# Node degrees of a graph layer as rows out of wide matmuls, in place of columns that are turned and copied

## The chip, the cores and the metric

The kernel runs on one core of a Trainium2 chip. The metric is device time in microseconds (us) of one execution. A change of 0.3% (2.3 us) either way is about what can be told from none.

## What is computed

3125 nodes with 256 features, 50,000 edges sorted by destination, and a layer norm with relu ahead of four SAGE layers:

```python
def _sage_conv(x, src, dst, Wl, Wr, b):
    n = x.shape[0]
    agg = jax.ops.segment_sum(x[src], dst, num_segments=n)
    deg = jax.ops.segment_sum(jnp.ones_like(dst, dtype=x.dtype), dst, num_segments=n)
    mean = agg / jnp.maximum(deg, 1.0)[:, None]
    return mean @ Wl + x @ Wr + b
...
h = jnp.maximum(_layernorm(x, axis=-1), 0.0)
x = x + gnn(h)      # relu after layers 1, 2 and 3
```

The change concerns `1 / maximum(deg, 1)`, which each layer multiplies into the summed neighbours.

## The kernel before

The edges are turned into a dense matrix `counts` (source by destination), kept in SBUF as 25 source tiles of 128 partitions with one column for each destination node. The sum over neighbours is then a matmul: `H` (two fp16 parts of the features) is the stationary operand, 512 columns of `counts` the moving one (`add_sources`, L1617).

Destinations are worked on in seven chunks, here called places q = 0 to 6. The order is written out by hand (`ORDER` = 5, 6, 4, 3, 2, 1, 0): place 0 is a chunk of 512 nodes, place 1 the last 53 nodes, places 2 to 6 have 512 nodes each. In layer 1 the matrix is built while it is used: in places 0 and 2 to 5, `script(q)` mixes two kinds of work over source tiles k = 0 to 24. One is the neighbour sum of this place (four 512-column matmuls for each k). The other is the building of `counts` for later places: VectorE (DVE) makes one-hot tables in pairs of instructions (`step`, L1061), TensorE (PE) multiplies them into `window_ps` (L1517), ScalarE (ACT) copies the result into `counts` (L1288). There are two buffers of tables (`GROUPS = 2`), so DVE can be at most two groups ahead of PE. Every engine works through its own list in the order in which it is written, and the engines meet at semaphores. Place 6 builds nothing.

The degrees of a place are made in four steps, before the sums of that place are scaled:

- `add_degrees` (PE, L1637): for each 128 nodes of the place, 25 matmuls with 128 columns of `counts` as the stationary operand and two columns of ones as the moving one. The result is a column in `lin_ps`. It is 100 matmuls for a place of 512 nodes and stands ahead of everything else in the place.
- `degrees` (DVE, L1143 and L1145): maximum with 1 and reciprocal on 128 partitions by 4, into `rdeg_columns`. PE waits for it at k = 1 (`degree_inverted`).
- `turn_degrees` (PE, L1649): four fp32 matmuls (two passes each, eight records) against an identity spread the columns over all partitions as rows in `degree_ps`, at k = 12 (k = 20 in place 0).
- `copy_degrees` (ACT, L1312): `degree_ps` to `rdeg`, 128 by 512.

In place 0, `degrees(0)` stands on DVE behind `choose_rest` (L907, tables of chosen steps) and far ahead of the steps. Near the end of layer 1 the DMA queue of SP stores the seven column tiles to `rdeg_d` in DRAM (`store_rdeg`, L609), and layers 2 to 4 load them from there as rows, spread over the partitions. `scale_agg` (L1117) multiplies by `rdeg`. In `script` terms, `lin` of the place before stands at k = 2, `narrow` at 10, `turn` at 18.

Of the kernel before, what the change touches and what calls it, by code (L numbers as in the profile page):

```python
# [26 lines left out]
def sage_stack_kernel(nc, x, src, dst, Wl1, Wr1, b1, Wl2, Wr2, b2, Wl3, Wr3, b3, Wl4, Wr4, b4, out):  # L27
# [13 lines left out]
    P = 128  # L41
# [3 lines left out]
    NT = -(-N // P)  # L45
    TAIL = N - (NT - 1) * P
    TPC = 4
# [153 lines left out]
    with ctx:  # L201
# [54 lines left out]
        norm_parts = uppers[:, 0:2 * NCH * TPC].rearrange("p (a c t) -> p a c t", a=2, c=NCH)  # L256
        rdeg_columns = uppers[:, 2 * NCH * TPC:3 * NCH * TPC].rearrange("p (q t) -> p q t", t=TPC)
        ident32 = uppers[:, 3 * NCH * TPC:3 * NCH * TPC + P]
# [160 lines left out]
        degree_inverted = sem("degree_inverted")  # L419
        degree_turned = sem("degree_turned")  # L420
        late_loaded = sem("late_loaded")
        rdeg_made = sem("rdeg_made")
        rdeg_stored = sem("rdeg_stored")
# [73 lines left out]
        REST_AT = {1: (0, 4, 9), 2: (0, 8), 3: (0, 7, 11)}  # L497
        DEGREE_TURN_K, DEGREE_COPY_K = 12, 13
        LIN_K, NARROW_K, TURN_K = 2, 10, 18
# [40 lines left out]
        def _(sp):  # L540
# [46 lines left out]
            for l in (1, 2, 3, 4):  # L587
# [17 lines left out]
                def store_rdeg(q):  # L605
                    c = ORDER[q]
                    n, t = size_of(c)
                    rows_ = P if n == CH else n
                    sp.dma_start(rdeg_d[0, c * CH:c * CH + n].rearrange("(t p) -> p t", p=rows_),  # L609
                                 rdeg_columns[0:rows_, q, 0:t], allow_slow_non_contiguous=True  # L610
                                 ).then_inc(rdeg_stored, 16)

# [69 lines left out]
                with sp.Fori(2, NCH - 2) as q:  # L682
                    after(q)
                if l == 1:
                    sp.wait_ge(degree_inverted, NCH)
                    for q in range(NCH):
                        store_rdeg(q)
                after(NCH - 2)
# [144 lines left out]
        def _(dve):  # L833
# [270 lines left out]
            def scale_agg(l, q, bank):  # L1104

                n, t = size_of(chunk_at(q))
                if l > 1:
                    dve.wait_ge(rdeg_loaded[l], 16 * (q + 1))
                else:
                    dve.wait_ge(rdeg_made, q + 1)  # L1110
                    if q == 0:
                        wait_h0T(dve)
# [26 lines left out]
            def degrees(q):  # L1139
                n, t = size_of(chunk_at(q))  # L1140
                rows_ = P if n == CH else n
# [90 lines left out]
        def _(act):  # L1232
# [159 lines left out]
            for q in range(NCH):  # L1392
# [3 lines left out]
                for kind, k in script(q):  # L1396
# [21 lines left out]
                    if q == 0 and k == 22:  # L1418
                        root_row(1)
                    if k == (DEGREE_COPY_K if q else FIRST_TURN_K + 1):  # L1420
                        copy_degrees(q)
                    if q >= 1 and k == RELU_K:
# [20 lines left out]
        def _(pe):  # L1443
# [179 lines left out]
            def add_degrees(q):  # L1623

                c = chunk_at(q)
                n, t = size_of(c)
                rows_ = P if n == CH else n
                if q == 0:
                    pe.wait_ge(h0T_copied, 8)
                elif q == 1:  # L1630
                    pe.wait_ge(h0T_copied, 2 * NCH)
                    pe.wait_ge(norms_made, 3)
                else:
                    pe.wait_ge(low_done[1], q - 1)
# [6 lines left out]
            def turn_degrees(q):  # L1641

                n, t = size_of(chunk_at(q))
                rows_ = P if n == CH else n
                pe.wait_ge(degree_inverted, q + 1)
                if q >= 1:
                    pe.wait_ge(rdeg_made, q)
                for i in range(t):
                    last = m(degree_ps[:, i * P:i * P + rows_], rdeg_columns[0:rows_, q, i:i + 1].broadcast_to([rows_, P]),  # L1649
                             ident32[0:rows_, 0:rows_], start=True, stop=True)  # L1650
                last.then_inc(degree_turned, 1)

# [22 lines left out]
            for q in range(NCH):  # L1675

                pe.wait_ge(window_stored, filled_after(q - 1))
                add_degrees(q)
                if q >= 1:
                    pe.wait_ge(agg_scaled[1], 2 * q)  # L1680
                for kind, k in script(q):
# [4 lines left out]
                    if kind != "sum":  # L1686
                        continue
                    if k == 1:
                        pe.wait_ge(degree_inverted, q + 1)
                    if q == 0 and k % TPC == 0:  # L1690
# [78 lines left out]
```

## Time and profile before

| | us |
|---|---|
| runs shown: median of 3 (lowest, highest) | 767.74 (765.6, 768.23) |
| profiled execution, its own time | 772.98 |
| its span, first to last instruction | 771.2 |
| mean granted TensorE clock | 0.944 |
| PE busy | 684.8 |
| DVE busy | 273.1 |
| ACT busy | 173.3 |
| POOL busy | 49.1 |

Busy time says how much an engine did, not what limited the kernel: the chain of waits (which work released which) and the stretches with their granted clock tell that. A granted clock of 1.00 is TensorE at 2.4 GHz, one of 0.50 is 1.2 GHz. Layer 1 lasts from about 66 to 399 us, layers 2 to 4 the rest.

### The profile page before, as it was taken

Reading aid. Unit: us, or ns where it says so; the run is one execution under the profiler, and the core shown is the slowest. Engines: PE = TensorE matmul, PEld = TensorE weight load, DVE = VectorE, ACT = ScalarE, POOL = GpSimd, SP = SyncE. Lnnn points to the kernel's source line nnn. Section 1 sums busy time; section 2 is a strip of 40 time slices with the busy share of each in tenths; the row PEclk is TensorE's granted clock in tenths of the full one; section 3 lists DMA queues with packets and bytes.
Section 4 is the critical chain, followed back from the end, with each engine's and each line's share of the span. In section 5 each row is a group of like instructions: output and inputs, shape, how many; then the busy total and the mean of one; then the engine's idle time right before and its main releaser. Section 6 shows DMA issues by size and latency. Waiting matters only on the chain.

```text
span 771.2 us, 11223 instructions
## 1 busy us (share of the span) xinstructions
PE 684.8 (89%) x4513; PEld 369.2 (48%) x4514; DVE 273.1 (35%) x627; ACT 173.3 (22%) x339; POOL 49.1 (6%) x91
## 2 busy tenths in 40 slices
PE   2637967899999999999996999989998999999997
PEld 1314544465555455455443444344443556466464
DVE  6696168168366475570101122122122101101001
ACT  4455166235163261130011001111211000000000
POOL 6213110000000000000000000000000101100100
PEclk9965989799899899999996999999999999999999
DMA  8011000010010100105342323422245330330230
GB/s 253 10 55 56 28 31 28 32 45 4 2 55 15 53 4 15 55 15 11 91 148 74 108 74 126 150 88 90 82 136 198 123 106 1 95 96 0 95 95 28
DMA packets 39422, 53.48 MB, mean 69 GB/s; under 512 B 8557, under 2 KB 21518, under 8 KB 39376
## 3 DMA queue, kind: packets, MB, share of 16 engines
q1 hardware_dynamic: 39260, 52.59, 22.4%
q8 instruction: 33, 0.54, 0.3%
q10 hardware_dynamic: 116, 0.24, 0.1%
q14 instruction: 13, 0.11, 0.0%
HBM read 31.86 MB, written 20.97 MB: 68 GB/s over the span
## 4 chain that ended last, share of the span: by engine, by line
PE 76%; DVE 13%; DMA 4%; ACT 3%; issue 2%; SPq 1%; DVEq 0%; POOL 0%; ACTq 0%; POOLq 0%
PE agg_ps L1617 35%; PE window_ps L1617 12%; PE lin_ps L1587 10%; PE window_ps L1517 6%; DVE early L1061 6%; PE lin_ps L1571 6%; PE lin_ps L1637 2%; PE turn_ps L1606 2%; PE lin_ps L1595 1%; DMA H_d<-newH 1%; DMA H<-H_d 1%; PE agg_ps L1663 1%; DVE counts L883 1%; ACT counts L1288 1%; PE window_ps L1454 1%
## 5 line engine op out<-in xcount | busy, mean ns | idle before, releaser
L1617 PE MATMUL agg_ps<-counts,H 128*128 128x512 f16 (+2 forms) x1500 | 361.6, 377 | 5.0 <-DMA H<-H_d 2.2
L1617 PEld LDWEIGHTS agg_ps<-counts,H 128*128 128x128 f16 x1500 | 130.3, 100 | 126.9 <-issue 13.9
L1061 DVE TENSOR_TENSOR early<-early 128x768 f16<-128x768 bf16 (+5 forms) x318 | 141.8, 500 | 69.7 <-PE window_ps L1517 68.5
L1517 PE MATMUL window_ps<-early 128*128 128x100 f16 (+1 forms) x892 | 101.8, 225 | 49.3 <-DVE early L1061 37.5
L1288 ACT ACTIVATE counts<-window_ps 128x400 f16<-128x400 f32 x196 | 97.1, 506 | 138.6 <-PE window_ps L1517 134.8
L1517 PEld LDWEIGHTS window_ps<-early 128*128 128x128 f16 x892 | 67.7, 102 | 125.8 <-issue 41.2
L1617 PE MATMUL window_ps<-counts,H 128*128 (+1 forms) x600 | 96.7, 317 | 0.0
L1617 PEld LDWEIGHTS window_ps<-counts,H 128*128 128x128 f16 x600 | 46.1, 99 | 49.5 <-issue 4.1
L800 POOL TENSOR_TENSOR newH<-newH,early 128x256 f32<-128x256 f32 (+1 forms) x25 | 17.4, 727 | 631.7 <-DMA newH<-in_x_dram 631.7
L1117 DVE SCALAR_TENSOR_TENSOR aggT<-agg_ps,columns,rdeg 128x512 f32<-128x512 f32 (+1 forms) x30 | 20.6, 716 | 97.2 <-PE agg_ps L1617 81.8
L1327 ACT ACTIVATE newT<-lin_ps,columns 128x512 f32<-128x512 f32 (+1 forms) x28 | 17.4, 633 | 120.8 <-PE lin_ps L1587 120.8
L1136 DVE COPY newH<-turn_ps 128x1024 f16<-128x1024 f16 (+1 forms) x28 | 17.7, 632 | 58.8 <-PE turn_ps L1606 58.8
L1124 DVE SCALAR_TENSOR_TENSOR partsT<-newT,columns,partsT 128x512 f16<-128x512 f32 (+1 forms) x21 | 14.3, 683 | 53.8 <-ACT partsT L1338 53.3
L1587 PE MATMUL lin_ps<-selfT,early 128*128 128x512 f32 (+1 forms) x56 | 26.8, 583 | 5.9 <-DMA W<-in_L_gnn_Wr_dram 4.9
L1207 DVE TENSOR_TENSOR newT<-lin_ps,newH 128x512 f32<-128x512 f32 (+1 forms) x13 | 8.7, 670 | 55.4 <-PE lin_ps L1571 55.4
L1571 PE MATMUL lin_ps<-W,aggT 128*128 128x256 f32 (+1 forms) x100 | 25.9, 382 | 1.7 <-DVE aggT L1117 1.7
L1587 PE MATMUL lin_ps<-aggT,W 128*128 128x512 f32 (+1 forms) x56 | 26.1, 590 | 1.2 <-DVE aggT L1117 1.2
L1571 PE MATMUL lin_ps<-W,selfT 128*128 128x256 f32 (+1 forms) x100 | 25.7, 379 | 0.0
L1587 PE MATMUL lin_ps<-selfT,W 128*128 128x512 f32 (+1 forms) x56 | 23.8, 547 | 0.0
L1327 ACT ACTIVATE newT<-newT,columns 128x512 f32<-128x512 f32 (+1 forms) x7 | 4.7, 667 | 84.0 <-DVE newT L1219 84.0
L1606 PE MATMUL turn_ps<-ident,partsT 128*128 128x128 f16 (+1 forms) x200 | 16.7, 227 | 5.4 <-DVE partsT L1124 5.4
L1571 PEld LDWEIGHTS lin_ps<-W,aggT 128*128 128x128 f32 (+1 forms) x100 | 18.5, 187 | 5.7 <-DVE aggT L1117 2.3
(138 smaller groups left out, 377.6 us busy)
## 6 DMA issues: line engine op xcount, KB each, us to landing
selfT<-hT_d SPq DMA_DIRECT2D x18, 512.0 KB, 4.3
hT_d<-newT SPq DMA_DIRECT2D x14, 512.0 KB, 4.1
rdeg<-rdeg_d SPq DMA_DIRECT2D x18, 256.0 KB, 4.2
counts<-in_x_dram SPq DMA_DIRECT2D x6, 512.0 KB, 6.9
H_d<-newH SPq DMA_DIRECT2D x12, 256.0 KB, 2.0
H<-H_d SPq DMA_DIRECT2D x12, 256.0 KB, 4.0
H_d<-newH SPq DMA_DIRECT2D x6, 512.0 KB, 2.6
H<-H_d SPq DMA_DIRECT2D x6, 512.0 KB, 5.2
```

What stands on the lines that cost most here:

```text
L800: nc.gpsimd.tensor_tensor(x4[0:q, i, :], x4[0:q, i, :], b4rows[0:q, :], ALU.add).then_inc(x4_biased, 1)
L1061: last = v.tensor_tensor(hot[:, group % GROUPS, 0:n * size].rearrange("p (r n d) -> p r n d", r=n, d=2), numbers_to[:, 0:size].rearrange(" ...
L1117: v.scalar_tensor_tensor(out=aggT[:, h, 0:n], in0=(agg_ps, window_ps)[bank][:, h, 0:n], scalar=unscale[:, l - 1:l], in1=rdeg[:, 0:n], op0= ...
L1136: v.tensor_copy(to, turn_ps[0:rows_, 0:2 * t, :].rearrange("p (t a) f -> p t a f", a=2)).then_inc(turn_copied[l], 1)
L1288: a.activation(counts[:, :, 2 * w * WIN:2 * (w + 1) * WIN].rearrange("p t (a w) -> p a t w", a=2), window_ps[:, FILL_AT[w] % 2, 0:2 * KEYS ...
L1327: a.activation(newT[:, h, 0:n], source, ACT.Relu, bias=bT[:, bias + h:bias + h + 1]).then_inc(relu_done[l], 1)
L1517: m(window_ps[:, at % 2, key0:key0 + keys], hot_src[:, group % GROUPS, r * P:(r + 1) * P], hot_key[:, group % GROUPS, r * keys:(r + 1) * k ...
L1571: last = m(lin_ps[0:rows_, g, i * D:(i + 1) * D], h, w, start=(j == 0), stop=(j == len(ops) - 1))
L1587: last = m(lin_ps[:, h, 0:n], w, r, start=(i == 0), stop=(i == len(ops) - 1))
L1606: last = nc.tensor.transpose(turn_ps[0:rows_, 2 * i + part, :], partsT[:, part, i * P:i * P + rows_], ident16[:, :])
L1617: last = m((agg_ps, window_ps)[bank][:, h, 0:n], H_of[:, k, part, h * P:(h + 1) * P], counts[:, k, chunk_cols(c, n)], start=first and part ...
L1637: last = m(lin_ps[0:rows_, 0, 2 * i:2 * i + 2], counts[:, k, bass.ds((c * TPC + i) * P, rows_)], ones16[:, 0:2], start=(k == 0), stop=(k = ...
```

## The change

`add_degrees` now has a 128 by 128 block of ones as the stationary operand and 512 columns of `counts` (53 in place 1) as the moving one. So every partition of `degree_ps` gets the whole row of degrees, with 25 matmuls for a place. `turn_degrees` and `copy_degrees` are gone, and so are PE's waits for `degree_inverted` at k = 1. `degrees` on DVE reads 128 by 512 from `degree_ps` and writes 128 by 512 into `rdeg`, the maximum and the reciprocal both on that shape. Since there is one `rdeg`, it first waits for the store of the row before it. In place 0 both the matmuls and the two DVE instructions stand at k = 20. The stores to `rdeg_d` are one row each and are issued place by place.

```diff
             def degrees(q):
                 n, t = size_of(chunk_at(q))
-                rows_ = P if n == CH else n
                 dve.wait_ge(degree_done, q + 1)
-                order.after(v.tensor_scalar(rdeg_columns[0:rows_, q, 0:t], lin_ps[0:rows_, 0, 0:2 * t].rearrange(
-                    "p (t a) -> p t a", a=2)[:, :, 0], 1.0, None, ALU.max))
-                v.reciprocal(rdeg_columns[0:rows_, q, 0:t], rdeg_columns[0:rows_, q, 0:t]).then_inc(degree_inverted, 1)
+                if q > 0:
+                    dve.wait_ge(rdeg_stored, 16 * q)
+                    dve.wait_ge(agg_scaled[1], 2 * q)
+                order.after(v.tensor_scalar(rdeg[:, 0:n], degree_ps[:, 0:n], 1.0, None, ALU.max))
+                v.reciprocal(rdeg[:, 0:n], rdeg[:, 0:n]).then_inc(degree_inverted, 1)
...
                     choose_rest()
-                    degrees(0)
                     h0_shift(5)
...
-                    if q >= 1 and k == DEGREE_K:
+                    if k == (DEGREE_K if q else FIRST_TURN_K):
                         degrees(q)
...
-            def copy_degrees(q):
-                n, t = size_of(chunk_at(q))
-                act.wait_ge(degree_turned, q + 1)
-                if q > 0:
-                    act.wait_ge(agg_scaled[1], 2 * q)
-                a.activation(rdeg[:, 0:n], degree_ps[:, 0:n], ACT.Copy).then_inc(rdeg_made, 1)
...
-                for i in range(t):
-                    for k in range(NT):
-                        last = m(lin_ps[0:rows_, 0, 2 * i:2 * i + 2], counts[:, k, bass.ds((c * TPC + i) * P, rows_)],
-                                 ones16[:, 0:2], start=(k == 0), stop=(k == NT - 1))
+                for k in range(NT):
+                    last = m(degree_ps[:, 0:n], ones16[:, 0:P], counts[:, k, chunk_cols(c, n)], start=(k == 0),
+                             stop=(k == NT - 1))
                 last.then_inc(degree_done, 1)
...
-                    if k == 1:
-                        pe.wait_ge(degree_inverted, q + 1)
...
-                    if k == (DEGREE_TURN_K if q else FIRST_TURN_K):
-                        turn_degrees(q)
+                    if q == 0 and k == FIRST_TURN_K:
+                        add_degrees(q)
...
                 def after(q, last=False):
 
+                    if l == 1:
+                        store_rdeg(q)
                     sp.wait_ge(lin_done[l], both(q + 1, LIN[l], 1 if l == 4 else LIN[l]))
```

On PE, at the start of place 0, the block of 100 matmuls stands ahead of the first sums. Before:

```order
L1552 ISA
L1637 MATMUL lin_ps<-newH,counts 128x2 x100
L1617 MATMUL agg_ps<-counts,H 128x512 x32
L1481 MATMUL lin_ps<-newH,counts 128x128 x8
L1617 MATMUL agg_ps<-counts,H 128x512 x4
```

Now:

```order
L1535 ISA
L1600 MATMUL agg_ps<-counts,H 128x512 x32
L1464 MATMUL lin_ps<-newH,counts 128x128 x8
L1600 MATMUL agg_ps<-counts,H 128x512 x4
```

The sums come first (L1617 of before is L1600 now), and the degree block has moved to k = 20, below.

On DVE, in the last third of place 0, six rows of one-hot tables (each pair is one group) and then `bound_h2` (`counts<-counts`). Before:

```order
L1061 TENSOR_TENSOR early<-early 128x768
L1061 TENSOR_TENSOR early<-early 128x600
L1061 TENSOR_TENSOR early<-early 128x768
L1061 TENSOR_TENSOR early<-early 128x600
L1061 TENSOR_TENSOR early<-early 128x768
L1061 TENSOR_TENSOR early<-early 128x600
L1016 TENSOR_SCALAR counts<-counts 128x128
```

Now:

```order
L1053 TENSOR_TENSOR early<-early 128x768
L1053 TENSOR_TENSOR early<-early 128x600
L1137 TENSOR_SCALAR rdeg<-degree_ps 128x512
L1138 RECIPROCAL rdeg<-rdeg 128x512
L1053 TENSOR_TENSOR early<-early 128x768
L1053 TENSOR_TENSOR early<-early 128x600
L1053 TENSOR_TENSOR early<-early 128x768
L1053 TENSOR_TENSOR early<-early 128x600
L1008 TENSOR_SCALAR counts<-counts 128x128
```

The two degree instructions now stand ahead of the last two groups and of everything behind them. PE's block of 25 stands at the same point, behind the first half of k = 20.

On PE, at the turn from place 1 to place 2 (as at the starts of places 3 to 5). Before:

```order
L1606 MATMUL turn_ps<-ident,partsT 128x128 x8
L1617 MATMUL agg_ps<-counts,H 128x53 x26
L1637 MATMUL lin_ps<-newH,counts 128x2 x100
L1617 MATMUL agg_ps<-counts,H 128x512 x2
L1517 MATMUL window_ps<-early 128x100 x4
```

Now:

```order
L1589 MATMUL turn_ps<-ident,partsT 128x128 x8
L1600 MATMUL agg_ps<-counts,H 128x53 x26
L1616 MATMUL degree_ps<-counts,newH 128x512 x25
L1600 MATMUL agg_ps<-counts,H 128x512 x2
L1500 MATMUL window_ps<-early 128x100 x4
```

The block keeps its place and changes its kind. Behind it PE has two matmuls of its own, and then needs a table from DVE, whose list has the two degree instructions first.

## Rows read from the trace of the kernel before

**Rows 1.** The page, busy us and share of the span, by engine.

```profile
PE 684.8 (89%) x4513; PEld 369.2 (48%) x4514; DVE 273.1 (35%) x627; ACT 173.3 (22%) x339; POOL 49.1 (6%) x91
```

**Rows 2.** Chain of waits, start of layer 1: start us, us, what.

```profile
66.38 5.49 DVE counts L907 x16
...
72.21 8.44 PE agg_ps L1617 x28
```

**Rows 3.** Timeline of PE there: start us, us, what, idle before and releaser.

```profile
66.54 2.80 PE L1637 MATMUL lin_ps<-newH,counts 128*128 128x2 f16 x100 [0.83 <-ACT newT L1267]
```

**Rows 4.** Windows: stretch, its us, busy by engine, then granted clock, DMA, GB/s.

```profile
76.00:78.00 2.00, 2.00 (x9) 0.89 (x8) 0.00 (x0) 0.00 (x0) 2.00 (x4) 0.81 0.00 0
```

**Rows 5.** Chain of waits, from place 1 into place 2.

```profile
156.09 2.49 PE lin_ps L1637 x100
...
158.98 0.84 DVE early L1061 x2
...
159.95 0.49 PE window_ps L1517 x4
```

**Rows 6.** Chain of waits, place 6.

```profile
369.81 0.89 PE degree_ps L1649 x8
370.70 5.18 PE agg_ps L1617 x24
```

**Rows 7.** Groups of DVE by shape: count, busy us, mean ns, idle before.

```profile
L1001 DVE TENSOR_TENSOR counts<-counts 128x256 f32<-128x256 f32 x2 | 0.8, 424 | 0.1
...
L1001 DVE TENSOR_TENSOR counts<-counts 128x128 f32<-128x128 f32 x1 | 0.3, 291 | 0.0
...
L1145 DVE RECIPROCAL newH<-newH 128x4 f32<-128x4 f32 x6 | 1.1, 178 | 0.2
...
L874 DVE RECIPROCAL newH<-newH 128x1 f32<-128x1 f32 x1 | 0.2, 165 | 2.4 <-ACT newH L1246 2.4
...
L1145 DVE RECIPROCAL newH<-newH 53x1 f32<-53x1 f32 x1 | 0.2, 155 | 0.0
```

**Rows 8.** One line's instructions: count, min, median, max ns, first and last start.

```profile
L874 DVE RECIPROCAL newH<-newH x7: 157/177/179, 13.3 to 100.8; 128x4 f32<-128x4 f32 x6, 128x1 f32<-128x1 f32 x1
```

**Rows 9.** Windows behind the degree blocks of places 2 to 5.

```profile
157.50:163.50 6.00, 5.29 (x71) 3.20 (x67) 3.89 (x10) 1.84 (x4) 0.00 (x0) 0.72 0.05 16
199.80:206.80 7.00, 6.42 (x37) 3.28 (x35) 3.89 (x10) 2.02 (x4) 0.00 (x0) 0.52 0.01 2
250.50:258.00 7.50, 6.70 (x37) 3.36 (x34) 3.89 (x10) 1.01 (x2) 0.00 (x0) 0.54 0.00 1
298.00:304.50 6.50, 5.50 (x114) 3.92 (x112) 3.94 (x10) 0.00 (x0) 0.00 (x0) 0.81 0.01 3
```

**Rows 10.** Timeline, last third of place 0, DVE.

```profile
121.56 1.92 DVE L1061 TENSOR_TENSOR early<-early 128x768 f16<-128x768 bf16 x4 [0.96 <-PE window_ps L1517]
123.39 0.28 DVE L1016 TENSOR_SCALAR counts<-counts 128x128 f32<-128x128 f32 x1
```

**Rows 11.** Timeline, last third of place 0, PE.

```profile
122.77 1.05 PE L1649 MATMUL degree_ps<-newH 128*128 128x128 f32 x8
```

**Rows 12.** Timeline of PE, an idle stretch ahead of place 0's steps.

```profile
103.62 0.82 PE L1517 MATMUL window_ps<-early 128*128 128x200 f16 x4 [4.61 <-DVE early L1061]
```

**Rows 13.** Windows, that stretch: the slices in which the clock changed.

```profile
100.00:101.00 1.00, 0.00 (x0) 0.00 (x0) 0.21 (x2) 0.63 (x2) 0.48 (x1) 0.82 0.00 0
107.00:108.00 1.00, 1.00 (x8) 0.88 (x7) 0.00 (x0) 0.51 (x2) 0.00 (x0) 0.77 0.00 0
```

**Rows 14.** Chain of waits, place 1.

```profile
139.57 1.31 PE lin_ps L1637 x25
...
141.38 0.45 PE agg_ps L1617 x6
```

**Rows 15.** Timeline of DVE, end of place 5, and of SP's queue behind it.

```profile
341.68 0.68 DVE L1136 COPY newH<-turn_ps 128x1024 f16<-128x1024 f16 x1
...
350.92 3.70 SPq L609 DMA_DIRECT2D rdeg_d<-newH  x7
```

More of the change, by code:

```diff
@@ L256, in sage_stack_kernel @@
         norm_parts = uppers[:, 0:2 * NCH * TPC].rearrange("p (a c t) -> p a c t", a=2, c=NCH)
-        rdeg_columns = uppers[:, 2 * NCH * TPC:3 * NCH * TPC].rearrange("p (q t) -> p q t", t=TPC)
         ident32 = uppers[:, 3 * NCH * TPC:3 * NCH * TPC + P]
@@ L419, in sage_stack_kernel @@
         degree_inverted = sem("degree_inverted")
-        degree_turned = sem("degree_turned")
         late_loaded = sem("late_loaded")
-        rdeg_made = sem("rdeg_made")
         rdeg_stored = sem("rdeg_stored")
@@ L497, in sage_stack_kernel @@
         REST_AT = {1: (0, 4, 9), 2: (0, 8), 3: (0, 7, 11)}
-        DEGREE_TURN_K, DEGREE_COPY_K = 12, 13
         LIN_K, NARROW_K, TURN_K = 2, 10, 18
@@ L605, in store_rdeg @@
                 def store_rdeg(q):
-                    c = ORDER[q]
+                    c = chunk_at(q)
                     n, t = size_of(c)
-                    rows_ = P if n == CH else n
-                    sp.dma_start(rdeg_d[0, c * CH:c * CH + n].rearrange("(t p) -> p t", p=rows_),
-                                 rdeg_columns[0:rows_, q, 0:t], allow_slow_non_contiguous=True
-                                 ).then_inc(rdeg_stored, 16)
+                    sp.wait_ge(degree_inverted, q + 1)
+                    sp.dma_start(rdeg_d[0:1, chunk_cols(c, n)], rdeg[0:1, 0:n]).then_inc(rdeg_stored, 16)
                 def store_new(q):
@@ L683, in _ @@
                     after(q)
[L684 to L687, printed above, removed]
                 after(NCH - 2)
@@ L1109, in scale_agg @@
                 else:
-                    dve.wait_ge(rdeg_made, q + 1)
+                    dve.wait_ge(degree_inverted, q + 1)
                     if q == 0:
@@ L1140, in degrees @@
                 n, t = size_of(chunk_at(q))
-                rows_ = P if n == CH else n
                 dve.wait_ge(degree_done, q + 1)
-                order.after(v.tensor_scalar(rdeg_columns[0:rows_, q, 0:t], lin_ps[0:rows_, 0, 0:2 * t].rearrange(
-                    "p (t a) -> p t a", a=2)[:, :, 0], 1.0, None, ALU.max))
-                v.reciprocal(rdeg_columns[0:rows_, q, 0:t], rdeg_columns[0:rows_, q, 0:t]).then_inc(degree_inverted, 1)
+                if q > 0:
[3 more added lines that the diff above has]
+                v.reciprocal(rdeg[:, 0:n], rdeg[:, 0:n]).then_inc(degree_inverted, 1)
             for i, w in enumerate(FILLS[-1]):
@@ L1419, in _ @@
                         root_row(1)
-                    if k == (DEGREE_COPY_K if q else FIRST_TURN_K + 1):
-                        copy_degrees(q)
                     if q >= 1 and k == RELU_K:
@@ L1626, in add_degrees @@
                 n, t = size_of(c)
[L1627 to L1630, printed above, removed]
+                if q > 0:
+                    pe.wait_ge(degree_inverted, q)
+                if q == 1:
                     pe.wait_ge(h0T_copied, 2 * NCH)
                     pe.wait_ge(norms_made, 3)
-                else:
-                    pe.wait_ge(low_done[1], q - 1)
-                for i in range(t):
-                    for k in range(NT):
-                        last = m(lin_ps[0:rows_, 0, 2 * i:2 * i + 2], counts[:, k, bass.ds((c * TPC + i) * P, rows_)],
-                                 ones16[:, 0:2], start=(k == 0), stop=(k == NT - 1))
-                last.then_inc(degree_done, 1)
-            def turn_degrees(q):
-                n, t = size_of(chunk_at(q))
-                rows_ = P if n == CH else n
-                pe.wait_ge(degree_inverted, q + 1)
[L1646 to L1651, printed above, removed]
+                for k in range(NT):
+                    last = m(degree_ps[:, 0:n], ones16[:, 0:P], counts[:, k, chunk_cols(c, n)], start=(k == 0),
+                             stop=(k == NT - 1))
+                last.then_inc(degree_done, 1)
             for i, w in enumerate(FILLS[-1]):
@@ L1677, in _ @@
                 pe.wait_ge(window_stored, filled_after(q - 1))
-                add_degrees(q)
+                if q == 0:
+                    pe.wait_ge(h0T_copied, 8)
                 if q >= 1:
+                    add_degrees(q)
                     pe.wait_ge(agg_scaled[1], 2 * q)
@@ L1687, in _ @@
                         continue
-                    if k == 1:
-                        pe.wait_ge(degree_inverted, q + 1)
                     if q == 0 and k % TPC == 0:
@@ L1705, in _ @@
                     add_sources(1, q, 0, k, k == 0, k == NT - 1, halves=(0,))
-                    if k == (DEGREE_TURN_K if q else FIRST_TURN_K):
-                        turn_degrees(q)
+                    if q == 0 and k == FIRST_TURN_K:
+                        add_degrees(q)
                     if q >= 1 and k == LIN_K:
```

## The prediction, made before the changed kernel ran

> **What bounds the kernel now.** I read the page first. PE is busy for 684.8 of 771.2 us and DVE for 273.1 [rows 1], but that is a mean over stages. The changed code lives in layer 1 alone, so I then followed the chain of waits from 60 to 400 us, and the timeline and the windows with their granted clock wherever the chain met a degree instruction. Five spots matter.
>
> *Start of place 0.* PE does the 100 small matmuls from 66.54 [rows 3], the four sums of k = 0, and then stands until DVE has done `choose_rest` (5.49 us from 66.38) and, behind it, `degrees(0)`. Only at 72.21 does PE go on with 28 sums, which take 8.44 us to 80.65 [rows 2]. The clock is at 1.2 GHz at first. In the window from 76 to 78 its mean is 0.81 [rows 4], so it rose at about 76.76 (0.5 for 0.76 us, 1.0 for 1.24).
>
> *Last third of place 0.* DVE sets the pace. It starts the groups that stand where the change inserts at 121.56 and the bounds behind them at 123.39, with no wait between [rows 10]. PE reaches k = 20 and turns the degrees at 122.77 [rows 11].
>
> *Starts of places 2 to 5.* Here both engines follow one another on the chain: degree block 2.49 us from 156.09 (to 158.58), DVE's two small instructions, a group of tables from 158.98, and PE's first step at 159.95 [rows 5]. The other three places read alike. Later in such a place PE is the fuller engine.
>
> *Place 6.* It builds nothing and PE is its bound: block, sums, and 0.89 us of turning, all on the chain [rows 6].
>
> *The clock.* Behind the degree blocks of places 2 to 5 it falls to 1.2 GHz. From the mean clocks 0.72, 0.52, 0.54 and 0.81 over 6.0, 7.0, 7.5 and 6.5 us [rows 9] the time at half speed is twice the missing share: 3.4, 6.7, 6.9 and 2.5 us, 19.5 in all. What PE did before each fall: 2.5 us of two-column matmuls and then some 0.6 to 1 us of waiting.
>
> **The change, part by part.**
>
> *The block of matmuls.* 24 sums of 512 columns take 5.18 us at full clock [rows 6], 0.216 each. The new block has 25 of that shape: 5.40 us against 2.49, so +2.91 in each place with 512 nodes. In place 1 (53 columns) I take old and new as equal.
>
> *The turning* goes: 8 records, −0.89 us on PE [rows 6], in the middle of a place where PE is the bound, so I credit it in full. ACT's copy goes as well. ACT waits for PE most of the time, so 0.
>
> *The maximum on 128 by 512.* An fp32 instruction of DVE goes from 291 ns at 128 columns to 424 at 256 [rows 7]: 1.04 ns a column over a base of 0.16 us, so 0.69 us for 512.
>
> *The reciprocal on 128 by 512* is the disputed price. No row shows it wide. Lower bound: a column costs it what it costs the instruction above, 0.69 us. Upper bound: L1145 goes from 155 ns at one column to 178 at four [rows 7], 7.7 ns a column, so 0.155 + 511 × 0.0077 = 4.1 us. L874 goes from 165 ns at one column [rows 7] to a median of 177 [rows 8], 4.0 ns a column and 2.2 us. These are differences of 12 and 23 ns, so weak, but both are well above 1.04. I take the mean slope, 5.85: 3.15 us.
>
> *Places 2 to 5.* What stands behind DVE's reciprocal is the first group of tables, and PE waits for that with only two sums of its own in hand. Block end to group start was 158.98 − 158.58 = 0.40 us [rows 5]. Now it is 0.69 + 3.15 + 0.07 for three hand-overs = 3.91, so +3.51. With +2.91 and −0.89 a place grows by 5.53; four: +22.1.
>
> *The last third of place 0.* PE reaches k = 20 at 122.77 and its block ends at 128.17. DVE's degree instructions then end at 132.06 or so. The groups that began at 121.56 [rows 10] begin 10.5 us later. DVE has no slack behind them, so +10.5. If the reciprocal is cheap (0.69), it is 8.0.
>
> *The start of place 0.* PE no longer does the block there and waits for nothing of DVE before k = 9, which needs `choose_rest` (71.87 at the latest, as now). So 32 sums start at 66.54. The clock rose 4.55 us after PE began to work without a pause (72.21 to 76.76). The same from 66.54 gives 71.09: 10.65 sums at 0.427 us, 21.35 at 0.216, end at 75.70 against 80.65: −4.95. Bounds: the rise stays at 76.76 (−2.1), or full clock from the first (−7.2). All that follows to 103 us hangs on PE's chain, so the gain is kept.
>
> *Place 1.* PE's wait at k = 1 goes: block end 140.88 to 141.38 [rows 14], −0.5.
>
> *Place 6.* +2.91 − 0.89 = +2.0. The reciprocal is hidden here: DVE is needed next only at k = 14. Were that cover gone, it would cost its 3.9 us.
>
> *The clock.* PE now has 4.5 us of waiting behind each block. There is one such row: PE stood for 4.61 us until 103.62 [rows 12], the clock fell at 100.64 and rose at 107.46 (from 0.82 and 0.77 in their slices [rows 13]), so 3.84 us at half speed after work began again, a loss of 1.9. Today's loss in places 2 to 5 is about (19.5 minus some 3 of waiting) / 2 / 4 = 2.1 each. So no change there, and +0.9 for place 0, which gets such a stretch for the first time, half of it under DVE.
>
> *The stores.* DVE now waits, before it overwrites `rdeg`, for the store of the row before it. SP issues that behind the store that follows `copy_turned`, at 341.68 in place 5, 8.8 us before `degrees(6)` [rows 15]; place 1 is tighter, but the block is now 5.4 us and covers it. 0. A store that landed later than that would hold DVE, and then PE, by the difference. The seven scattered stores (3.70 us of SP's queue, [rows 15]) had nothing behind them on SP but a wait for `lin` of place 5, which PE does only after that. 0.
>
> Sum: −4.95 + 10.5 + 0.9 − 0.5 + 22.1 + 2.0 = +30.05 us. The profiled execution would go from 773.0 to 803. It lies 0.7% above the median of the runs shown, 767.7, and on the median the sum gives 797.8.
>
> **The rivals.**
>
> *The reciprocal is as cheap as a copy.* Then DVE's part is 2.46 shorter in five places, and PE waits only 2 us behind each block, which is now full-width work, so that the clock may stay up: −4.95 + 8.0 − 0.5 + 4 × 3.07 + 2.0 = +16.8, and −8.3 for the clock (4 × 2.1): +8.5, 776; 784 if the clock falls all the same. For it: a pipeline that overlaps its passes. Against: both slopes of rows 7 and 8.
>
> *The reciprocal costs 4.1 to 4.4 and the clock stays down longer.* +1.0 to +1.25 in five places, and +1 in each for the clock: 808. For it: the slope of L1145. Against: that of L874.
>
> *The change is faster.* Mechanism: the clock. The wide block keeps it up behind all four blocks (−8.3) and through place 1, which starts at 1.2 GHz today (−2.3). It decides only if DVE's two instructions also lie fully under PE's work, so that just PE's terms are left: five places × 2.02 and 4.5 in place 0 = 14.6. With −4.95 and −0.5: −1.5, 766. Against it: in places 2 to 5 PE has 0.43 us of work of its own behind the block, and DVE's cheapest case is 1.45.
>
> *No net change*: the same without place 1, 768.
>
> **How the numbers follow.** Chances: forecast (797.8) 0.70, own range 789 to 804; longer reciprocal 0.12; cheap reciprocal 0.13 and the same without the clock's help 0.02; faster 0.02; no change 0.01. The range 776 to 806 leaves out most of the longer case and the last two. A change under 0.3%, 2.3 us, can't be told from none. Faster 0.02, same 0.01, slower 0.97.
>
> **What the new profile would show.** Right: RECIPROCAL 128 by 512 near 3.1 us; the block 25 times 0.216; PE idle for about 4.5 us behind it in places 2 to 5, released by the tables; the sums at the start of place 0 without a pause and the matmuls of the first select (L1454 of before) 5 us earlier; the bounds in the last third of place 0 about 5.5 us later than now (10.5 less the lead). Wrong: a reciprocal of 0.7 us, or a clock at 1.00 behind the blocks, or DVE waiting for a DMA ahead of its maximum.

## The result, and the profile after

The changed kernel takes 800.5 us (median of 4, 799.7 to 803.1) against 766.7: ratio 1.044, 95% interval 1.041 to 1.047, so +33.8 us. The forecast was 797.8 and +30. The profiled execution took 799.72 us with a span of 797.9.

The page of the changed kernel, part 1 (busy time by engine):

```profile
PE 693.8 (87%) x4013; PEld 362.2 (45%) x4014; DVE 294.5 (37%) x627; ACT 170.4 (21%) x332; POOL 49.1 (6%) x91
```

Against [rows 1], PE has 9.0 us more and DVE 21.4 more. Neither sum tells what the 33.8 us are. The groups of DVE by shape do half of it (count, busy us, mean ns, idle before):

```profile
L1138 DVE RECIPROCAL rdeg<-rdeg 128x512 f32<-128x512 f32 x6 | 20.1, 3353 | 0.2
L1137 DVE TENSOR_SCALAR rdeg<-degree_ps 128x512 f32<-128x512 f32 x6 | 4.2, 692 | 30.2 <-PE degree_ps L1616 30.2
L1138 DVE RECIPROCAL rdeg<-rdeg 128x53 f32<-128x53 f32 x1 | 0.5, 490 | 0.0
```

The reciprocal takes 3.353 us where I had 3.15. From 53 to 512 columns it is (3353 − 490) / 459 = 6.24 ns a column, six times the 1.04 ns of [rows 7]. The maximum takes 0.692, the forecast to the digit. DVE stood 30.2 us ahead of the maxima, waiting for PE's blocks.

The chain of waits from place 1 into place 2 answers to [rows 5]:

```profile
160.03 5.41 PE degree_ps L1616 x25
165.46 0.70 DVE rdeg L1137
166.19 3.35 DVE rdeg L1138
169.54 0.80 DVE early L1053 x2
170.47 0.49 PE window_ps L1500 x4
```

All three new terms are on it, one behind the other: block 5.41, maximum 0.70, reciprocal 3.35, and only then the first group of tables that PE waits for. PE's timeline at the same spot shows the wait:

```profile
170.47 0.49 PE L1500 MATMUL window_ps<-early 128*128 128x100 f16 x4 [4.62 <-DVE early L1053]
```

The last third of place 0, timeline of DVE, against [rows 10]:

```profile
123.12 0.69 DVE L1137 TENSOR_SCALAR rdeg<-degree_ps 128x512 f32<-128x512 f32 x1 [7.76 <-PE degree_ps L1616]
123.85 3.35 DVE L1138 RECIPROCAL rdeg<-rdeg 128x512 f32<-128x512 f32 x1
127.12 1.72 DVE L1053 TENSOR_TENSOR early<-early 128x768 f16<-128x768 bf16 x4
128.76 0.28 DVE L1008 TENSOR_SCALAR counts<-counts 128x128 f32<-128x128 f32 x1
```

DVE stands 7.76 us and then works 4.04 on degrees. And the start of place 0, timeline of PE, against [rows 2, 3]:

```profile
64.67 9.53 PE L1600 MATMUL agg_ps<-counts,H 128*128 128x512 f16 x32 [0.88 <-ACT newT L1259]
74.04 1.04 PE L1464 MATMUL lin_ps<-newH,counts 128*128 128x128 f32 x8
```

The 32 sums run in one go. The windows behind the blocks of places 2 to 5 (stretch, busy by engine, then granted clock, DMA share, GB/s) answer to [rows 9]:

```profile
168.00:176.50 8.50, 6.03 (x35) 4.04 (x36) 5.05 (x9) 2.01 (x4) 0.00 (x0) 0.60 0.00 0
219.50:224.00 4.50, 4.50 (x24) 2.50 (x22) 2.31 (x6) 2.01 (x4) 0.00 (x0) 0.62 0.01 4
274.00:278.50 4.50, 3.50 (x23) 2.10 (x24) 3.24 (x9) 0.50 (x1) 0.00 (x0) 0.62 0.00 0
328.50:333.50 5.00, 4.44 (x26) 2.60 (x27) 3.14 (x8) 0.00 (x0) 0.00 (x0) 0.66 0.00 0
```

By twice the missing share they hold 6.8, 3.4, 3.4 and 3.4 us at 1.2 GHz, 17.0 in all. For the kernel before, the prediction read 19.5 from [rows 9]. The last of those windows ends too early: in place 5 the clock is still down behind it (0.69 from 304.5 to 306), so it was 3.4 us there, not 2.5, and some 20.5 in all.

Measured from block to block (and in place 6 to the start of the last `lin`), the places took, before and after: place 0 73.0 and 79.55, place 1 16.5 and 15.8, place 2 41.4 and 48.7, place 3 50.7 and 55.8, place 4 49.65 and 54.1, place 5 50.1 and 55.7, place 6 35.2 and 37.2. Together that is 316.6 and 346.9 us, +30.3 in layer 1.

### The profile page after: what moved, and what is told of

It is laid out like the page before. It is cut to its first block, busy times and chain, and to the rows that moved or that the text cites. A ratio compares the mean times of both kernels' runs of the same rounds, so it can differ in the third digit from the quotient of the medians.

```text
span 797.9 us, 10217 instructions
## 1 busy us (share of the span) xinstructions
PE 693.8 (87%) x4013; PEld 362.2 (45%) x4014; DVE 294.5 (37%) x627; ACT 170.4 (21%) x332; POOL 49.1 (6%) x91
## 4 chain that ended last, share of the span: by engine, by line
PE 76%; DVE 14%; ACT 3%; DMA 2%; issue 2%; POOL 1%; SPq 1%; ACTq 0%; DVEq 0%; POOLq 0%
PE agg_ps L1600 34%; PE window_ps L1600 11%; PE lin_ps L1570 9%; DVE early L1053 6%; PE lin_ps L1554 5%; PE window_ps L1500 5%; PE degree_ps L1616 4%; DVE rdeg L1138 2%; PE turn_ps L1589 2%; PE lin_ps L1578 1%; POOL counts L709 1%; DMA H_d<-newH 1%; ACT counts L1280 1%; PE lin_ps L1464 1%; DVE counts L875 1%
## 5 line engine op out<-in xcount | busy, mean ns | idle before, releaser
L1600 PE MATMUL agg_ps<-counts,H 128*128 128x512 f16 (+2 forms) x1500 | 360.0, 376 | 4.1 <-DMA H<-H_d 1.8
L1600 PEld LDWEIGHTS agg_ps<-counts,H 128*128 128x128 f16 x1500 | 131.0, 100 | 126.0 <-issue 15.0
L1600 PE MATMUL window_ps<-counts,H 128*128 (+1 forms) x600 | 96.2, 316 | 0.0
L1600 PEld LDWEIGHTS window_ps<-counts,H 128*128 128x128 f16 x600 | 45.6, 98 | 49.6 <-issue 4.1
L1109 DVE SCALAR_TENSOR_TENSOR aggT<-agg_ps,columns,rdeg 128x512 f32<-128x512 f32 (+1 forms) x30 | 20.5, 715 | 96.8 <-PE agg_ps L1600 81.6
L1128 DVE COPY newH<-turn_ps 128x1024 f16<-128x1024 f16 (+1 forms) x28 | 17.7, 632 | 56.6 <-PE turn_ps L1589 56.6
L1616 PE MATMUL degree_ps<-counts,newH 128*128 128x512 f16 (+1 forms) x175 | 34.6, 357 | 1.6 <-issue 1.6
L1116 DVE SCALAR_TENSOR_TENSOR partsT<-newT,columns,partsT 128x512 f16<-128x512 f32 (+1 forms) x21 | 14.3, 683 | 54.1 <-ACT partsT L1323 53.6
L1554 PE MATMUL lin_ps<-W,selfT 128*128 128x256 f32 (+1 forms) x100 | 25.7, 379 | 0.0
L1616 PEld LDWEIGHTS degree_ps<-counts,newH 128*128 128x128 f16 x175 | 15.8, 101 | 19.5 <-issue 2.0
```

The source lines that it names most:

```text
L1109: v.scalar_tensor_tensor(out=aggT[:, h, 0:n], in0=(agg_ps, window_ps)[bank][:, h, 0:n], scalar=unscale[:, l - 1:l], in1=rdeg[:, 0:n], op0= ...
L1128: v.tensor_copy(to, turn_ps[0:rows_, 0:2 * t, :].rearrange("p (t a) f -> p t a f", a=2)).then_inc(turn_copied[l], 1)
L1554: last = m(lin_ps[0:rows_, g, i * D:(i + 1) * D], h, w, start=(j == 0), stop=(j == len(ops) - 1))
L1600: last = m((agg_ps, window_ps)[bank][:, h, 0:n], H_of[:, k, part, h * P:(h + 1) * P], counts[:, k, chunk_cols(c, n)], start=first and part ...
L1616: last = m(degree_ps[:, 0:n], ones16[:, 0:P], counts[:, k, chunk_cols(c, n)], start=(k == 0), stop=(k == NT - 1))
```

## The experiments

**1. The kernel before once more.** The profiled execution of before lay 6 us above the median of its runs, so 3.5 us of the measured 33.8 had no place in the comparison above.

> The kernel before once more, unchanged, with a profile of its own. Its profiled execution (772.98 us) lay 6 us above the median of its runs (766.7), while that of the changed kernel lay at its median. Theory: the extra 4 to 6 us is spread between executions (head of the program, clock), so a new profile near 767 should show layer 1 from PE's first sum to the last agg scaled within 2 us of the 317 us of the first profile, and the rest elsewhere. Rival: the first profile had an extra stall inside layer 1, and then the new one shows layer 1 shorter by 3 to 6 us, so that the change costs more there than the 30.2 us that the two profiles show. Time against before: same, 766 to 768.

Measured: 766.9 us, ratio 1.000 (0.997 to 1.003). Its profile has a span of 766.4, and layer 1 takes 313.4 us, not 316.6. The rival holds: the first profile had 3.2 us more inside layer 1. Windows of this profile, behind the blocks of places 2 to 5:

```profile
155.00:162.00 7.00, 6.35 (x132) 4.39 (x128) 4.04 (x12) 1.32 (x3) 0.00 (x0) 0.76 0.12 40
196.00:205.00 9.00, 8.00 (x135) 5.22 (x133) 5.21 (x12) 2.01 (x4) 0.00 (x0) 1.00 0.02 5
247.00:255.00 8.00, 7.00 (x55) 3.83 (x52) 3.89 (x10) 1.01 (x2) 0.00 (x0) 0.79 0.01 3
295.00:303.00 8.00, 7.00 (x83) 4.29 (x81) 3.89 (x10) 0.00 (x0) 0.00 (x0) 0.79 0.00 0
```

In place 3 the clock did not fall at all, and in place 4 for 3.4 us in place of 6.9: 10.1 us at half speed against some 20.5 in the first profile, with the same program. Places 2 to 5 took 41.4, 48.4, 48.7 and 50.0 us here (41.4, 50.7, 49.65 and 50.1 in the first profile). Against this profile the change costs 33.5 us in layer 1, close to the 33.8 of the medians.

**2. Without the reciprocal.** The values are then not means.

```diff
-                v.reciprocal(rdeg[:, 0:n], rdeg[:, 0:n]).then_inc(degree_inverted, 1)
+                v.tensor_scalar(rdeg[:, 0:n], rdeg[:, 0:n], 0.001, None, ALU.min).then_inc(degree_inverted, 1)
```

> The changed kernel with the wide reciprocal (3.353 us) replaced by a wide minimum with 0.001 on the same tile, so the scaled values are not the means; everything else is as it was. Theory (the reciprocal is on the path in places 0 and 2 to 5): the wide minimum takes about 0.43 us, so 2.9 less in five places, -14.6: 786 us. If PE's shorter wait (about 2 us in place of 5) also keeps its clock at 2.4 GHz behind the blocks, about 7 us more are gained: 779. Rival (the wait behind the block is not the reciprocal's but the tables', or the time comes back as a wait elsewhere): 797 to 801.

Measured: 779.1 us, 21.4 less than the changed kernel (ratio to before 1.016, 1.010 to 1.022). The wide minimum takes 0.426 us, so 2.93 less in each of five places, 14.6. Most of the other 6.8 goes with the clock: in the profiles, places 2 to 5 are 17.7 us shorter together, 11.7 of which is the reciprocal, and the remaining 5.9 come where 17.0 us at 1.2 GHz are gone. Windows of this run behind the same four blocks:

```profile
163.00:169.50 6.50, 4.75 (x42) 3.17 (x40) 4.61 (x10) 2.01 (x4) 0.00 (x0) 1.00 0.00 0
206.50:213.50 7.00, 5.19 (x33) 2.60 (x32) 4.61 (x10) 2.01 (x4) 0.00 (x0) 1.00 0.01 2
258.00:265.00 7.00, 5.19 (x32) 2.61 (x31) 4.61 (x10) 1.01 (x2) 0.00 (x0) 1.00 0.01 4
308.00:315.00 7.00, 4.93 (x32) 2.46 (x31) 4.61 (x10) 0.00 (x0) 0.00 (x0) 1.00 0.00 0
```

The clock is at 1.00 throughout. So this run is close to the case that the prediction called the cheap reciprocal (776): its second instruction is cheaper still, 0.43 and not 0.69, and it comes out 3 us above that.

**3. A block of 12 source tiles.** The degrees are then too small.

```diff
-                for k in range(NT):
+                for k in range(12):
...
-                             stop=(k == NT - 1))
+                             stop=(k == 11))
```

> The changed kernel with the degree block cut to 12 of its 25 source tiles, so the degrees are too small; the DVE instructions are the same. 12 matmuls of 512 columns take 2.6 us, as long as the old block. Theory (PE's block is on the path in all six places of 512 nodes): -2.8 in each, -16.8 in all: 784 us. Rival (in places 0 and 2 to 5 the block is covered, because DVE has table groups left to build): -2.8 in place 6 alone: 797.

Measured: 784.5 us, 16.0 less than the changed kernel (ratio to before 1.023, 1.017 to 1.029). 13 matmuls of 0.216 us in six places are 16.8. In the profiles the six places are shorter by 2.7, 3.1, 3.0, 1.8, 2.8 and 2.8 us, so the block is on the path everywhere, not in place 6 alone. (In the one with 1.8, place 4, this run has 6.8 us at 1.2 GHz and the changed kernel 3.4.)

**4. Place 0's inverse at the end of the place.**

```diff
                     if kind == "summed":
+                        if q == 0:
+                            degrees(0)
                         scale_agg(1, q, 0)
...
-                    if k == (DEGREE_K if q else FIRST_TURN_K):
+                    if q >= 1 and k == DEGREE_K:
```

> The changed kernel with the two DVE degree instructions of place 0 moved from k = 20 to the end of place 0, just ahead of the scaling of its sums; PE's block stays at k = 20. Theory (at k = 20 DVE stands 7.8 us for PE's block and then works 4.1 us at the degrees, while PE has nothing to do, and this costs 10.6 us): now DVE goes on while the block runs, is late by the block alone (4.5 us net of the turning that went), and the 4.1 us come back at the end of the place, partly under PE's block of place 1: 8 us in place of 10.6, so -2 to -4: 797 to 798.5. Rival (DVE sets the pace in all of the last third of place 0, so where the work stands makes no difference): within 1 us of 800.5.

Measured: 794.5 us, 6.0 less than the changed kernel, more than I expected. Place 0 takes 73.3 us, what it took before the change. The timeline of DVE in this run shows why:

```profile
117.04 1.91 DVE L1053 TENSOR_TENSOR early<-early 128x768 f16<-128x768 bf16 x4 [0.96 <-PE window_ps L1502]
118.87 0.28 DVE L1008 TENSOR_SCALAR counts<-counts 128x128 f32<-128x128 f32 x1
...
124.54 1.80 DVE L1053 TENSOR_TENSOR early<-early 128x768 f16<-128x768 bf16 x4 [3.06 <-PE window_ps L1502]
```

DVE has built its two groups at about 118.9, just as PE begins its block (118.24 to 123.8), goes through the bounds beneath the block, and so stands for 3.06 us, not 7.76. I had counted the block as a full delay of DVE and forgotten the 2.6 us of bounds that fit beneath it. Of the reciprocal, 2.82 us come back as PE's wait ahead of the block of place 1.

**5. The start lead alone, on the kernel before.** The gain at the start of place 0 does not need wide rows.

```diff
-                add_degrees(q)
                 if q >= 1:
+                    add_degrees(q)
                     pe.wait_ge(agg_scaled[1], 2 * q)
...
-                    if k == 1:
+                    if k == 1 and q > 0:
                         pe.wait_ge(degree_inverted, q + 1)
+                    if q == 0 and k == 14:
+                        pe.wait_ge(degree_inverted, 1)
...
                     if q == 0 and k == FIRST_STEPS_K:
+                        add_degrees(0)
                         pe.wait_ge(step_tables, 4)
...
                     choose_rest()
-                    degrees(0)
...
                     more_tables(2)
+                    degrees(0)
```

> The kernel before with one edit: the 100 small matmuls of place 0 and the wait for them leave the start of place 0 and stand at k = 13, where PE waits 4.6 us for DVE's first tables; DVE's two small degree instructions stand behind the last step tables. Theory (the start lead of the changed kernel, 4.6 us, comes only from PE's missing block and wait, and does not need wide rows): 766.5 - 4.6 = 762 us, with PE's first sums running without a pause. Rival (the lead is lost again, because the clock falls on the small matmuls or DVE is held up ahead of the first tables): 765 to 767.

Measured: 763.2 us against 767.1 (ratio 0.994, 0.992 to 0.997), faster than both kernels: 3.9 of the expected 4.6 us. PE's timeline in this run:

```profile
65.48 8.55 PE L1617 MATMUL agg_ps<-counts,H 128*128 128x512 f16 x32
...
90.26 2.64 PE L1637 MATMUL lin_ps<-newH,counts 128*128 128x2 f16 x100
97.00 0.83 PE L1517 MATMUL window_ps<-early 128*128 128x200 f16 x4 [3.65 <-DVE early L1061]
```

The block lies where PE waits for DVE anyway, and PE still waits 3.65 us behind it, so it costs nothing there. This edit is in runs 6, 9 and 10 as well.

**6. The small block spread over the place.** Run 5, and the 100 small matmuls of places 1 to 6 in ten parts:

```diff
-        LOW_K, DEGREE_K, COPY_K = 14, 0, 20
+        LOW_K, DEGREE_K, COPY_K = 14, 11, 20
...
                 if q >= 1:
-                    add_degrees(q)
                     pe.wait_ge(agg_scaled[1], 2 * q)
...
-                    if k == 1 and q > 0:
-                        pe.wait_ge(degree_inverted, q + 1)
...
+                    if q >= 1 and k < SPREAD:
+                        some_degrees(q, k)
```

> As e5_block0_in_gap, and in places 1 to 6 the block of small matmuls no longer stands ahead of the place but is spread in ten parts over k = 0 to 9, into the free bank degree_ps; DVE's two small instructions stand at k = 11 and nothing waits at k = 1. Theory (at the start of a place the small block costs more than its 2.5 us of PE: DVE stands through it, PE then waits for tables, and the clock falls to 1.2 GHz for 3.4 to 6.8 us in most places): about 1 us less of waiting and 1 to 1.5 us less for the clock in each of places 2 to 5, -8 to -10 against e5_block0_in_gap: 753 us. Rival (the small matmuls cost more between large ones, or DVE waits at k = 11 instead): 760 to 763.

Measured: 766.8 us (ratio 0.999, 0.997 to 1.001), 14 more than the theory said. The small matmuls are hardly dearer (ten take 0.25 us from the first to the next large one, as in the block; only the first ten of places 2 to 5 take 0.42), and the clock stays at 1.00 in places 2 to 5. Two other things ate the gain. First, timeline of PE at the start of place 6 (it is the same at the starts of places 3, 4 and 5, and 0.69 us in place 2):

```profile
337.06 0.59 PE L1619 MATMUL agg_ps<-counts,H 128*128 128x512 f16 x2 [1.26 <-DVE aggT L1118]
```

PE now waits for the scaling of the place before, which the block had covered: 5.7 us in the five places. From scaling to scaling, places 2 to 5 are 4.7 us shorter than in run 5, where 8 to 10 were expected, and place 6 is 1.5 longer. Second, the end of place 6 (timeline, SP's queue and PE):

```profile
355.37 3.43 SPq L610 DMA_DIRECT2D rdeg_d<-newH  x7
...
358.84 0.58 SPq L597 DMA_DIRECT2D selfT<-hT_d  x1
...
377.61 2.90 PE L1589 MATMUL lin_ps<-aggT,W 128*128 128x512 f32 x3 [6.29 <-DMA selfT<-hT_d]
```

The seven scattered stores now stand directly ahead of the load of `selfT`, since `degree_inverted` comes later in place 6, and that load took 18.6 us to land. PE stood 6.3 us for it.

**7. The wide reciprocal in pieces.** The changed kernel, maximum at k = 3 and eight pieces at k = 4 to 18 in places 2 to 6:

```diff
+            def invert(q, i):
+                cols = slice(i * CH // 8, (i + 1) * CH // 8)
+                last = v.reciprocal(rdeg[:, cols], rdeg[:, cols])
...
+                    if q >= 2 and k % 2 == 0 and 4 <= k <= 18:
+                        invert(q, k // 2 - 2)
```

> The changed kernel, but in places 2 to 6 the maximum stands at k = 3 and the reciprocal is cut into eight pieces of 64 columns at k = 4, 6, ... 18, between the groups of tables. A piece should take 0.16 + 64 x 0.00624 = 0.56 us, 4.5 us in all. Theory (DVE is idle for some 17 us of such a place, so pieces that are shorter than the two groups it may be ahead are covered): 4 us less in four places, and PE waits only for the first tables, so the clock stays up, about 7 us more: 777 us. Rival (DVE's lead is too short, PE waits for each piece): 795 to 802.

Measured: 778.6 us, 21.9 less than the changed kernel. The forty pieces take 0.538 us each, 21.0 us in all, more than the 16.8 of the five whole reciprocals that they replace, and are covered. DVE's busy time is 292.7 us, almost that of the changed kernel, so it was never the amount of work that cost, but its place. The maximum moved along with the reciprocal, and the clock stays at 1.00 in places 2 to 5, so the 21.9 are worth all three together.

**8. The wide reciprocal under the next block.** The changed kernel, reciprocal at the end of places 0 and 2 to 5, and a semaphore of its own for PE once the maximum is through:

```diff
                     if kind == "summed":
+                        if q not in (1, NCH - 1):
+                            invert(q)
                         scale_agg(1, q, 0)
...
-                    if k == (DEGREE_K if q else FIRST_TURN_K):
+                    if k == {0: 22, 1: 0}.get(q, 3):
...
-                    pe.wait_ge(degree_inverted, q)
+                    pe.wait_ge(degree_read, q)
```

> The changed kernel, but in places 0 and 2 to 5 the reciprocal stands at the end of the place, just ahead of the scaling, and the maximum at k = 3 (k = 22 in place 0); PE's next block waits only until the maximum has read degree_ps. Theory (3.35 us of reciprocal and 1.4 us of scaling fit under the next block of 5.4 us, which stood idle for DVE before): 4 us less in four places and 7 us less for the clock, and 6 to 8 us less in place 0, as in e4_place0_inverse_last and with no wait of place 1's block: 770 to 772 us. Rival (the time comes back at the end of the place, because the scaling and lin behind it are now late): 785 to 795.

Measured: 768.3 us (ratio to before 1.001, 0.999 to 1.003), 32 less than the changed kernel, and no different from the kernel before. The three parts of the edit (reciprocal, maximum, semaphore) were not run one by one. Timeline at the start of place 3:

```profile
191.64 3.34 DVE L1145 RECIPROCAL rdeg<-rdeg 128x512 f32<-128x512 f32 x1
...
194.44 5.56 PE L1625 MATMUL degree_ps<-counts,newH 128*128 128x512 f16 x25
195.02 1.41 DVE L1110 SCALAR_TENSOR_TENSOR aggT<-agg_ps,columns,rdeg 128x512 f32<-128x512 f32 x2
...
196.35 1.78 DVE L1054 TENSOR_TENSOR early<-early 128x768 f16<-128x768 bf16 x4
199.84 0.59 PE L1609 MATMUL agg_ps<-counts,H 128*128 128x512 f16 x2
```

The scaling and the first two groups of tables lie under the block and are done by 198.13, and PE goes from its block to the next sum at 199.84 without a wait. The reciprocal lies mostly ahead of the block: 2.8 of its 3.34 us pass while PE still does the last sums of place 2 (191.64 to 194.44), and 2.0 to 2.8 us at the ends of places 3 to 5. So the theory had the cover in part wrong: the last sums of a place cover the reciprocal, which the early semaphore allows, and the block covers what follows it.

**9. Run 6 with the stores place by place.**

```diff
+                    if l == 1:
+                        sp.wait_ge(degree_inverted, q + 1)
+                        store_rdeg(q)
...
                 if l == 1:
-                    sp.wait_ge(degree_inverted, NCH)
-                    for q in range(NCH):
-                        store_rdeg(q)
+                    for q in range(2, NCH - 2):
+                        after(q)
```

> As e6_block_spread, but the column stores to rdeg_d are issued place by place instead of seven in a row. In e6_block_spread the profile shows PE standing 6.3 us in place 6 for selfT, whose load took 18.6 us because it queued behind the seven scattered stores, and then 6.8 us at 1.2 GHz. Theory (that stall, not the small matmuls, ate what the spreading had won): 6.3 + 3.4 = 9.7 us less, 757 us. Rival (small matmuls between large ones, and the wait for the scaling at the start of a place, are what ate it): 764 to 767.

Measured: 760.8 us against 766.0 (ratio 0.993, 0.991 to 0.996), 6.0 less than run 6, or 4.9 when each is taken against the kernel before of its own session. The load of `selfT` lands in 4.2 us and PE's 6.3 us of standing are down to 1.22, so the theory holds in kind. The size falls 3.7 us short of the 9.7 that I had added up, and the profiles show why. At that spot PE waits 1.22 us for the scaling in this run too. And of the 6.8 us at 1.2 GHz in run 6, PE stood through the first 2.9, so the other 3.9 cost 2.0, not 3.4. That leaves 5.1 + 2.0 = 7.1 us; behind layer 1 the two profiles differ by 7.4.

**10. Half of the small block ahead, half spread.**

```diff
                 if q >= 1:
+                    some_degrees(q, -1)
                     pe.wait_ge(agg_scaled[1], 2 * q)
```

> As e9_spread_stores_by_place, but half of each block (50 small matmuls, 1.25 us) stands at the start of the place again, ahead of PE's wait for the scaling of the place before; the other half is spread over k = 0 to 9. In e6_block_spread PE waited 1.26 us there, which the block had covered. Theory: 1.25 us less in each of five places, -5 to -6 against e9_spread_stores_by_place: 751 us. Rival (the small matmuls at the start bring the clock down again, as the whole block did): the same as e9_spread_stores_by_place or 2 us more.

Measured: 756.4 us against 766.0 (ratio 0.988, 0.985 to 0.991), 4.4 less than run 9, where 5 to 6 were expected, and the fastest kernel here. (The 751 of the theory was counted from 757, the forecast for run 9.) The 50 small matmuls take the place of the wait:

```profile
190.33 1.41 DVE L1121 SCALAR_TENSOR_TENSOR aggT<-agg_ps,columns,rdeg 128x512 f32<-128x512 f32 x2 [2.58 <-PE agg_ps L1622]
190.47 1.39 PE L1643 MATMUL degree_ps<-newH,counts 128*128 128x2 f16 x50
```

## Why the prediction was right

**Blocks.** Forecast 5.40 us, measured 5.41, on the path in all six places of 512 nodes (run 3).

**Place 6**, +2.0: measured 37.23 − 35.22 = +2.01. Block and turning are both confirmed there, the turning credited in full, and the reciprocal is hidden.

**Maximum and reciprocal.** 0.69 and 3.15 forecast, 0.692 and 3.353 measured. The mean of the two slopes from one to four columns, 5.85 ns, came close to the measured 6.24; the lower slope (4.0) and the upper (7.7) would have missed by about a third and a fifth. That it came so near is luck. The lower slope set 177 ns, a median over both shapes of L874, against 165. The mean of its six instructions of 128 by 4 is 172 in the same trace, so like for like it is 2.3 ns, the mean of the two slopes 5.0, and the reciprocal 2.7 us. What the rows did carry is that a column of a reciprocal costs more than twice the 1.04 ns of the other instruction. The rule of the Trainium skill (VectorE: DVE Perf Modes, section on the 8-slice pipeline in each mode) read as eight passes for each column gave, as an estimate, 4.4 us; measured are 3.353 us, and a column takes the time of six and not of eight. Why six, no run here shows. That the cost of the reciprocal and the maximum lay in PE's wait for tables is shown by runs 2, 7 and 8, which take it away in three ways.

**Places 2 to 5**, +22.1: the two first profiles show +22.4. That agreement owes something to chance. Block end to group start is 169.54 − 165.44 = 4.10 us against 0.40, so +3.70 and, with the block and the turning, 5.7 a place, 22.9. Against run 1 the four places grew by 25.7 (7.3, 7.3, 5.3 and 5.7). The remaining 2.8 go with the clock: in places 4 and 5 both profiles have 3.4 us at 1.2 GHz, and the growth is near the 5.7 of the other terms; in places 2 and 3 the changed kernel has 3.4 us more of it than run 1, and each grew by 1.6 more than 5.7. That is the term that was mis-sized: I took "today's loss" of 2.1 us a place from one profile and set the change at nought. The same program in run 1 spent 10.1 us at half speed in the four places, not 19.5 (or 20.5, as read above), while the changed kernel spent 17.0. Here the forecast fell short by 3.6 us, 0.8 of it the dearer reciprocal and 2.8 the clock.

**Last third of place 0**, +10.5: the bounds moved from 0.62 us behind PE's arrival at k = 20 [rows 10, 11] to 11.2 behind it (117.53 to 128.76), +10.6, of which 9.9 reached the start of place 1's block. The size was right; the reason, as put ("DVE has no slack behind them"), left out that DVE had useful work to do under the block, had it only been allowed to go on (run 4).

**Start of place 0**, −4.95: from PE's start to the transposes behind the 32 sums, 13.95 us before and 9.37 now, −4.6 (the clock rose 5.0 us after PE's start, not 4.55). Run 5 shows such a lead without any wide row (8.38 us there). Of it 1.2 us were gone again at k = 20: the clock came back to 2.4 GHz 6.7 us after the first steps (97.17 to 103.84), not 3.84 us as in [rows 12, 13]. I had kept the gain whole. The +0.9 for a new stretch at 1.2 GHz behind the block of place 0 was right in kind (0.66 from 127 to 132, 3.4 us at half speed). The place as a whole was forecast at −4.95 + 10.5 + 0.9 = +6.45 and grew by 6.55, with errors in its terms that cancel.

**Place 1**, −0.5: −0.7. **The stores**, 0: right, and with less room than I thought. In the first profile the load of `selfT` behind the scattered stores took 12.6 us to land and was due 11 us after that; run 6 shows what happens when it is not.

**The rivals.** The faster case needed DVE's two instructions under PE's work and the clock up, in place 1 as well (766); without place 1 it was the case of no net change, at 768. Run 8 is that one: no wait behind the block, the clock at 1.00 in places 2 to 5 but at 1.2 GHz for 10.2 us at the end of place 0 and in place 1, and 768.3 us. Against run 1, place 0 is 1.6 us shorter, places 1 to 5 are together as long as before, and place 6 is 2.0 longer. So the start lead and what the clock gives back are used up by the longer blocks (2.0 us more of PE in a place, net of the turning).

## What to carry to other kernels

Ahead of moving a small result to a wide one, price each instruction at its new width on the engine that hands out the next work: here 4 us on DVE, between the block and the first tables, were on the path in four places and put hardly anything on it once they stood beside work that PE had of its own, the last sums and the next block (run 8). Where such work must be done, look for a stretch in which the other engine has long work of its own, and give the buffer a semaphore that frees it as soon as its last reader is through. A block of small matmuls is worth splitting between a wait that it can fill and the body of the place (run 10), and worth keeping out of the start of a chain (run 5). A term that one profile shows, such as time at the lower clock, needs a second profile of the same program before its change is set at nought (run 1).

## What the runs showed of the hardware that I had not expected

DVE's reciprocal costs 6.24 ns a column in fp32 (0.490 us at 53 columns, 0.538 at 64, 3.353 at 512), where a maximum or minimum on 512 columns takes 0.692 from PSUM and 0.426 from SBUF.

The clock behind the same block is not the same in every execution: in place 3 of the same program it was at 1.2 GHz for 6.7 us in one profile and never in another. What came before the falls were 2.5 us of two-column matmuls and a short wait, or 4.6 us of waiting. Neither 5.4 us of 512-column matmuls with 1.8 us of waiting (run 2) nor small matmuls spread among large ones (run 6) were followed by one in places 2 to 5.

Scattered stores of 4 bytes an element hold up what is queued behind them far beyond their own size. The seven hold 12.5 KB, and a 512 KB load behind them took 12.6 us to land when it was issued 4.9 us after the last of them, 14.0 us likewise in run 1, and 18.6 us directly behind, against 4.4 in the changed kernel and 4.2 in run 9, which have none there.
